# VectorE instead of GpSimd splits the queries and keys of batch 1 in layer 1 into bfloat16 parts

## The chip, the cores and the metric

The kernel runs on one NeuronCore of a Trainium2 chip. The metric is the device time of one execution in microseconds, a median over several runs. TensorE is called PE in the profile, VectorE DVE, ScalarE ACT, GpSimd POOL; SyncE (SP) issues nearly all DMAs. PEld is PE's weight load. Each engine works through its own instruction list in order, and they meet at semaphores.

## The reference

Two layers on x of shape (4, 512, 256) in float32: batch, tokens, channels. Each layer is x = layernorm(x + attention(x)), then x = layernorm(x + ffn(x)).

Layer 0 has attention with 16 query and 4 key heads, RMS norm and rotary embedding, and a mixture of 8 experts (one per token) beside a shared expert. Layer 1 has causal attention with 16 heads of 16 channels and a dense MLP whose weights are 4-bit integers with scales, plus low-rank terms. The part of the change is the start of layer 1's attention:

```
qkv = x @ W_qkv.T + b_qkv
q, k, v = split(qkv, 3)              # to 16 heads of 16 channels
scores = einsum('bnqd,bnkd->bnqk', q, k) * 16 ** -0.5
scores = where(causal, -inf, scores)
attn = softmax(scores)
out = einsum('bnqk,bnkd->bnqd', attn, v)
```

## The kernel before

**Splitting into bfloat16 parts.** The scores are wanted to nearly float32 precision but computed with bfloat16 matmuls. A float32 tile is taken apart into three bfloat16 parts: part 0 is the value rounded to bfloat16, the remainder is the value less part 0, part 1 is the remainder rounded, part 2 is the remainder less part 1. The parts of Q and K are written to DRAM and read back stacked, six rows per channel (96 rows for 16 channels), so that one bfloat16 matmul of 96 rows holds the products of the parts that matter.

**Units of work.** The order of all work is written out by hand as one string of step names. Every engine goes through that same string and does its own share of each step. In layer 1, for batch b:

- `cX`: PE turns the rows of x, ACT copies them.
- `cQ0` to `cQ3`: PE makes a 128 x 512 tile (`products`, L676); even ones are Q, odd ones K; two halves of the heads. ACT evicts it twice (L1108), with the bias: once as float32 to `qf`, once as bfloat16 to part 0 of `cparts`. ACT's step waits until split i-2 is done, and from i = 2 on for the DMAs that wrote the parts of the same buffer to DRAM before.
- `cK0` to `cK3`: the split of tile i: subtract, copy, subtract. For batches 0, 2 and 3 it is on DVE (L1469 to L1471), for batch 1 on POOL (L1609 to L1613). SP then writes the parts to DRAM in three DMAs (L643) and after every second split reads the stacks back (L628); the second half of batch 1's stacks is read only in `cM0`.
- `max` (written `m`): PE makes one bank of scores of the row maxima's pass, with the causal mask added by a second matmul (L904, L906); DVE reduces it to the row maxima (L1496). A batch has 44 such steps, over 512 or 384 columns.
- `cm`: DVE copies the finished maxima into two bfloat16 parts (L1503, L1504). `cM`: PE turns them, ACT copies them (L1124), SP writes them by two DMAs as two more rows of the Q stacks (L650), so that the second pass subtracts the maximum within the matmul.
- `cattS`, `cattP`: the 16 attention steps of a batch: scores (L928), exponential on ACT (L1118), the triangle cleared on POOL (L1622), the product with the values (L941).
- `Wul`, `Wdl`: low-rank products added to the dequantised MLP weights; ACT evicts, POOL adds (L1598).

**Order around the change.** The maxima of batch 0 have nothing of layer 1's attention to hide behind and run in the open, with Q and K of batch 1 among them (`+` marks batch 1, `m` without sign batch 0):

```
cX m m m m +cQ0 +cK0 m m m m m m +cQ1 +cK1 m m m m m m +cQ2 +cK2
m m m m m m m +cQ3 +cK3 m m m Wdl0 m m m m Wdl1 m m m Wdl2 m (11 times)
cm0 +cV0 Wd3 >cL0 >cL1 cM0 Wdl3 +cV1 >cE0     then the attention steps of batch 0
```

Maxima of batch 0 take turns over four PSUM banks (`WIDE`), since the score banks are still free; all other steps of this kind share three (`UNITS`). PE waits before a maximum until DVE has reduced the one that had the bank (`take`). Maxima of batches 1 to 3 lie between attention steps of the batch before.

The semaphore `cparts_ready` counts finished splits of either engine. On POOL the three instructions of a split wait for each other by `pool_parts`; on DVE `link` does that.

Of the kernel before, what the change touches and what calls it, by code (L numbers as in the profile page):

```python
# [25 lines left out]
ALU = mybir.AluOpType  # L26
# [124 lines left out]
def post_ln_layers(nc, ins, out):  # L151
# [4 lines left out]
    with ExitStack() as ctx:  # L156
# [5 lines left out]
        def place(shape, dt=F32):  # L162

            n = int(np.prod(shape)) * (2 if dt == BF16 else 4)
            n = (n + 31) // 32 * 8
            at = top[0]
            top[0] += n
            assert top[0] <= words, (top[0] * 4, words * 4)
            ap = arena[:, at:at + n]
            if dt != F32:  # L170
                ap = ap.bitcast(dt)
            ap = ap[:, 0:int(np.prod(shape))]
            if len(shape) > 1:
                names = "abcd"[:len(shape)]
                ap = ap.rearrange(f"p ({' '.join(names)}) -> p {' '.join(names)}",
                                  **{x: s for x, s in zip(names[1:], shape[1:])})
            return ap
# [156 lines left out]
        cresid = place([S])  # L334
# [4 lines left out]
        cparts = place([2, 3, S], BF16)  # L339
        qf = [place([S])]  # L340
# [19 lines left out]
        def sem(name):  # L360
            return ctx.enter_context(nc.semaphore(name))
# [60 lines left out]
        cparts_ready = sem("cparts_ready")  # L422
# [2 lines left out]
        cs_stack = [[sem(f"cstacks_loaded{h}{i}") for i in range(2)] for h in range(HG)]  # L425
        m_parts = sem("max_parts_ready")
        s_m = sem("max_rows_loaded")
        pool_parts = sem("pool_parts_chain")
        kones = sem("k_ones_ready")
        x3_ready = sem("x3_ready")  # L430
        y_ready = sem("y_ready")
# [8 lines left out]
        def yrow_of(b):  # L440

            return c_a_t.rearrange("p c (h n) -> p (c h) n", n=C) if b == 1 else yrow
# [37 lines left out]
        def consumed(eng, step):  # L480

            if step[:2] == OPENING:
                eng.wait_ge(max_free[step[2] % WIDE], step[2] // WIDE + 1)
                return
            u = unit_no[step]
            eng.wait_ge(unit_free[u % UNITS], u // UNITS + 1)
# [648 lines left out]
        def _(v):  # L1135
# [98 lines left out]
            for step in a_steps:  # L1234
                n, b, i = step
# [199 lines left out]
            for step in c_steps:  # L1435
                n, b, i = step
# [21 lines left out]
                elif n == "cE":  # L1458
                    tiles = x_sb[:, NT * b:NT * b + NT, :]
                    normalise(tiles, tiles, 0, NT, x2_ready, 2 * b + 2)  # L1460
                elif n == "cK" and b != 1:

                    s = i % 2
                    consumed(v, ("cQ", b, i))
# [71 lines left out]
        @block.gpsimd  # L1536
        def _(pool):

            pool.wait_ge(score_ready, 1)
            pool.wait_ge(s_xs, 16 * (B - 1))  # L1540
            nc.gpsimd.tensor_tensor(xs, x_sb[:, NT * (B - 1):NT * B, :], score.unsqueeze(2).to_broadcast([P, NT, C]),  # L1541
                                    ALU.mult).then_inc(xs_ready, 1)
            consumed(pool, ("ID", 0, 0))
            pool.wait_ge(s_xs, 16 * B)
            for j in range(MT):
                if j == 2:
                    consumed(pool, ("D", B - 2, 0))
                    consumed(pool, ("D", B - 2, 1))
                    nc.gpsimd.memset(low_rank, 0.0).then_inc(zeroed, 1)
                if j >= 2:  # L1550
                    pool.wait_ge(xgt_ps, j - 1)
                nc.gpsimd.indirect_dma_start(out=xg[:, j % 2, :], out_offset=None, in_=xs_dram,
                                             in_offset=bass.IndirectOffsetOnAxis(ap=ids[:, j:j + 1], axis=0))\
                  .then_inc(xg_in[j % 2], 16)

            pool.wait_ge(s_nat, 16 * 10)
            nc.gpsimd.tensor_scalar(n_up, n_up.bitcast(I32), 7.5, None, ALU.subtract).then_inc(poolc, 1)
            pool.wait_ge(poolc, 1)
            up4 = n_up.rearrange("p r (k j) -> p (r k) j", j=BLOCK)
            nc.gpsimd.tensor_tensor(up4, up4, n_ups.rearrange("p r k -> p (r k)").unsqueeze(2)  # L1560
                                    .to_broadcast([P, NK * C // BLOCK, BLOCK]), ALU.mult).then_inc(deq, 1)
            pool.wait_ge(deq, 1)
            nc.gpsimd.tensor_scalar(n_dn, n_dn.bitcast(I32), 7.5, None, ALU.subtract).then_inc(poolc, 1)
            pool.wait_ge(poolc, 2)
            dn4 = n_dn.rearrange("p r (k j) -> p (r k) j", j=BLOCK)
            nc.gpsimd.tensor_tensor(dn4, dn4, n_dns.rearrange("p r k -> p (r k)").unsqueeze(2)
                                    .to_broadcast([P, 2 * HID // BLOCK, BLOCK]), ALU.mult).then_inc(deq, 1)
            pool.wait_ge(deq, 2)

            pool.wait_ge(y_st[0], 16 * (MT // 2 + 1))  # L1570
            pool.wait_ge(y_st[1], 16 * (MT // 2))
            pool.wait_ge(y_full, MT)

            def gather(b):
                for t in range(NT):
                    nc.gpsimd.indirect_dma_start(out=yrow_of(b)[:, t, :], out_offset=None, in_=yg_dram,
                                                 in_offset=bass.IndirectOffsetOnAxis(ap=slot_i[:, NT * b + t:NT * b + t + 1],
                                                                                     axis=0)).then_inc(gathered[b % 2], 16)

            gather(0)  # L1580
            gather(1)
            for step in c_steps:
                n, b, i = step
                if n == "cL" and i == 1 and b == 1:

                    pool.wait_ge(x2_ready, 2)
                    gather(2)
                if n == "cP" and i == 1 and b == 0:

                    pool.wait_ge(x2_ready, 2 * B - 2)  # L1590
                    gather(B - 1)
                if n in ("Wul", "Wdl"):
                    k = low_steps.index(step)
                    consumed(pool, (n[:2], 0, i))
                    consumed(pool, step)
                    dst = (w_up[:, i // 2, 512 * (i % 2):512 * (i % 2 + 1)] if n == "Wul" else
                           w_dn[:, 2 * i:2 * i + 2, :].rearrange("p r n -> p (r n)"))
                    nc.gpsimd.tensor_tensor(dst, low_sum[k % 2], dst, ALU.add).then_inc(low_added, 1)  # L1598
                if n == "Wdl" and i < 2:
                    consumed(pool, ("cX", 0, i))  # L1600
                    pool.wait_ge(s_bias, 48)
                    rows = x_sb[:, 2 * i:2 * i + 2, :]
                    nc.gpsimd.tensor_tensor(rows, rows, bo_b.unsqueeze(1).to_broadcast([P, 2, C]), ALU.add).then_inc(o_bias, 1)
                if n == "cK" and b == 1:

                    t = i % 2
                    consumed(pool, ("cQ", b, i))
                    pool.wait_ge(cparts_ready, 4 * b + i)
                    nc.gpsimd.tensor_tensor(cresid, qf[t], cparts[:, t, 0, :], ALU.subtract).then_inc(pool_parts, 1)  # L1609
                    pool.wait_ge(pool_parts, 2 * i + 1)  # L1610
                    nc.gpsimd.tensor_copy(cparts[:, t, 1, :], cresid).then_inc(pool_parts, 1)
                    pool.wait_ge(pool_parts, 2 * i + 2)
                    nc.gpsimd.tensor_tensor(cparts[:, t, 2, :], cresid, cparts[:, t, 1, :], ALU.subtract)\  # L1613
                      .then_inc(cparts_ready, 1)
                elif n == "cattS":

                    k = head0 * B + headc * b + i
                    kt = i % NT
                    pool.wait_ge(exp_done[0], k + 1)
                    pool.wait_ge(exp_done[1], k + 1)  # L1620
                    diag = cprobs[:, i % 2, :, P * kt:P * (kt + 1)]
                    nc.gpsimd.affine_select(out=diag, in_=diag, compare_op=ALU.is_ge, fill=0.0, base=0,  # L1622
                                            pattern=[[0, 4], [1, P]], channel_multiplier=-1).then_inc(masked, 1)
# [35 lines left out]
def build(nc, arrays):  # L1659
    args = {n: nc.dram_tensor(f"in_{n}", a.shape, mybir.dt.from_np(a.dtype), kind="ExternalInput").ap()  # L1660
            for n, a in arrays.items()}
    out = nc.dram_tensor("out_0", (B, S, C), F32, kind="ExternalOutput").ap()
    post_ln_layers(nc, args, out)
# [24 lines left out]
```

## Time and profile before

| | us |
|---|---|
| median of 3 runs | 808.87 (807.51 to 809.41) |
| profiled execution | 804.52 |
| its span | 802.8 |
| PE busy | 755.4 (94%) |
| DVE busy | 446.9 (56%) |
| ACT busy | 398.7 (50%) |
| POOL busy | 126.8 (16%) |

The span is the time from the first to the last instruction of the profiled execution. Busy times overlap between engines. Times in rows are microseconds from the start of the span.

### The profile page before, as it was taken

What the parts mean: (1) busy time and instruction counts of PE and PEld (TensorE: products, weight loads), DVE (VectorE), ACT (ScalarE), POOL (GpSimd) and SP (SyncE); (2) the same over time, 40 slices, a digit from 0 to 9 for tenths busy, and PEclk for the clock granted to TensorE, in tenths of its full rate; (3) what the DMA queues carried; (4) which work ended last, traced back from release to release, by engine and by line L of the source; (5) the groups of instructions that cost most, each with busy time, mean ns of one, the idle gap of its engine ahead of it and who ended that gap; (6) DMA issues with size and microseconds to landing.
All of it is one profiled execution on the core that took longest, in us unless ns stands there. A gap on an engine that the chain in (4) does not pass through costs nothing. (4 is left out here: it accounts for less than half of the span.)

```text
span 802.8 us, 12486 instructions
## 1 busy us (share of the span) xinstructions
PE 755.4 (94%) x4393; PEld 446.3 (56%) x4394; DVE 446.9 (56%) x1194; ACT 398.7 (50%) x593; POOL 126.8 (16%) x135
## 2 busy tenths in 40 slices
PE   8899999999999999999999897989989998999996
PEld 4323434444434589999977554435445644653685
DVE  4663744565354722222228798939685667563464
ACT  3499775786595154454525325465333453146230
POOL 0000000000000131111563372223101110022100
PEclk9999999999999999999999999989999999999999
DMA  7668116105106262111123882005600280000000
GB/s 230 182 204 280 43 35 191 51 27 155 42 27 218 72 183 76 46 52 46 39 70 109 242 260 81 2 2 153 189 1 3 79 234 6 26 1 27 0 27 27
DMA packets 53822, 75.03 MB, mean 93 GB/s; under 512 B 7926, under 2 KB 45082, under 8 KB 53386
## 3 DMA queue, kind: packets, MB, share of 16 engines
q1 hardware_dynamic: 51900, 69.26, 28.0%
q0 software_dynamic: 1872, 5.11, 2.4%
q8 instruction: 30, 0.49, 0.3%
q14 instruction: 20, 0.16, 0.1%
HBM read 46.57 MB, written 27.66 MB: 92 GB/s over the span
## 5 line engine op out<-in xcount | busy, mean ns | idle before, releaser
L676 PE MATMUL ps<-arena 128*128 128x256 f32 (+3 forms) x1084 | 315.8, 439 | 5.6 <-DVE arena L1217 1.4
L676 PEld LDWEIGHTS ps<-arena 128*128 128x128 f32 x1084 | 196.1, 190 | 87.9 <-issue 55.4
L1003 ACT ACTIVATE arena<-ps 128x1024 f32<-128x1024 f32 x128 | 124.1, 1029 | 25.6 <-PE ps L744 25.3
L1118 ACT ACTIVATE arena<-ps 128x1024 f32<-128x1024 f32 (+3 forms) x128 | 82.9, 702 | 99.0 <-PE ps L928 98.8
L1496 DVE TENSOR_REDUCE arena<-ps 128x1 f32<-128x384 f32 (+3 forms) x176 | 100.5, 634 | 26.0 <-PE ps L906 25.3
L806 PE MATMUL ps<-arena 128*128 128x128 f32 x736 | 89.4, 275 | 0.6 <-DVE arena L1228 0.6
L806 PEld LDWEIGHTS ps<-arena 128*128 128x128 f32 x736 | 87.4, 192 | 2.4 <-issue 1.3
L1622 POOL TENSOR_SCALAR_AFFINE_SELECT arena<-arena 128x512 f32<-128x512 f32 x64 | 42.5, 664 | 218.4 <-ACT arena L1118 218.4
L904 PE MATMUL ps<-arena 96*128 96x128 bf16 (+3 forms) x256 | 62.3, 306 | 12.0 <-DVE arena L1496 7.3
L744 PE MATMUL ps<-arena 96*128 96x512 bf16 x256 | 69.7, 382 | 4.2 <-ACT arena L1003 2.7
L758 PE MATMUL ps<-arena 128*32 128x512 f32 x512 | 68.8, 604 | 0.3 <-ACT arena L1010 0.3
L744 PEld LDWEIGHTS ps<-arena 96*128 96x128 bf16 x256 | 17.8, 97 | 77.5 <-ACT arena L1003 40.7
L928 PE MATMUL ps<-arena 98*128 98x512 bf16 (+3 forms) x256 | 47.8, 307 | 4.9 <-ACT arena L1118 2.7
L941 PE MATMUL ps<-arena 128*32 128x128 f32 (+3 forms) x512 | 49.0, 454 | 2.8 <-POOL arena L1622 1.8
L906 PE MATMUL ps<-arena 128*128 128x128 bf16 x256 | 49.5, 223 | 0.0
L904 PEld LDWEIGHTS ps<-arena 96*128 96x128 bf16 x256 | 25.3, 99 | 39.0 <-DVE arena L1496 19.6
L928 PEld LDWEIGHTS ps<-arena 98*128 98x128 bf16 x256 | 18.2, 98 | 47.6 <-issue 31.4
L1541 POOL TENSOR_TENSOR arena<-arena 128x1024 f32<-128x1024 f32 x1 | 1.9, 1895 | 265.7 <-DVE arena L1326 265.7
L815 PE MATMUL ps<-arena 128*128 x184 | 43.4, 379 | 0.0
L1031 ACT ACTIVATE arena<-ps 128x512 f32<-128x512 f32 x23 | 13.7, 597 | 55.8 <-PE ps L806 55.8
L668 PE MATMUL ps<-arena 128*128 128x128 f32 (+3 forms) x237 | 33.9, 280 | 7.7 <-DVE arena L1270 3.2
L668 PEld LDWEIGHTS ps<-arena 128*128 128x128 f32 (+3 forms) x237 | 28.1, 141 | 20.5 <-issue 8.6
(160 smaller groups left out, 755.3 us busy)
## 6 DMA issues: line engine op xcount, KB each, us to landing
arena<-stacks_dram SPq DMA_DIRECT2D x32, 384.0 KB, 6.3
arena<-in_gate_up_proj SPq DMA_DIRECT2D x8, 1024.0 KB, 9.3
stacks_dram<-arena SPq DMA_DIRECT2D x16, 384.0 KB, 3.7
arena<-in_down_proj SPq DMA_DIRECT2D x8, 512.0 KB, 9.0
stacks_dram<-arena SPq DMA_DIRECT2D x16, 256.0 KB, 4.0
q_stacks_dram<-arena SPq DMA_DIRECT2D x8, 384.0 KB, 3.3
arena<-q_stacks_dram SPq DMA_DIRECT2D x8, 384.0 KB, 4.8
arena<-q_stacks_dram SPq DMA_DIRECT2D x4, 768.0 KB, 5.8
```

Source lines behind the costliest of these rows:

```text
L668: last = nc.tensor.transpose(dst[0:rows, col:col + n], src, idn)
L676: last = nc.tensor.matmul(dst[0:rows, lo:hi], a, w, start=(n == 0), stop=(n == len(pairs) - 1))
L744: last = nc.tensor.matmul(ps[:, g, :], k_stack[0:STACK, b % 2, hg, cols(kt)], q_stack[0:STACK, b % 2, 4 * hg + g, :], start=True, stop=True)
L758: last = nc.tensor.matmul(ps[32 * g:32 * g + 32, 4, :], v_aug[:, kt, hg, :], (probs0, probs1)[i % 2][:, g, :], start=(kt == 0), stop=(kt = ...
L806: last = nc.tensor.matmul(ps[:, 2 * half + up, cols(f)], of_expert[:, up, c, cols(f)], xg_t[:, half, c, :], start=(c == 0), stop=(c == 1))
L904: nc.tensor.matmul(dst[:, w * g:w * (g + 1)], cq_stack[0:STACK, b % 2, h0 + g, cols(qt)], ck_stack[0:STACK, b % 2, h0 + g, 0:w], start=Tru ...
L906: last = nc.tensor.matmul(dst[:, w * g + P * qt:w * (g + 1)], identb, negmask, start=False, stop=True, skip_group_check=True)
L928: last = nc.tensor.matmul(ps[:, g, P * kt:S], ck_stack[0:STACK + 2, b % 2, h, cols(kt)], cq_stack[0:STACK + 2, b % 2, h, P * kt:S], start= ...
L941: last = nc.tensor.matmul(ps[32 * g:32 * g + 32, 4, P * kt:S], cv_aug[:, b % 2, kt, 4 * hg + g, :], cprobs[:, i % 2, g, P * kt:S], start=( ...
L1003: nc.scalar.activation(probs[:, 2 * p:2 * p + 2, :], ps[:, 2 * p:2 * p + 2, :], ACT.Exp)\
L1118: nc.scalar.activation(cprobs[:, i % 2, 2 * p:2 * p + 2, P * kt:S], ps[:, 2 * p:2 * p + 2, P * kt:S], ACT.Exp).then_inc(exp_done[p], 1)
L1496: nc.vector.tensor_reduce(mneg[:, qt, h0:h0 + nh], filled(v, step)[:, 0:nh * w].rearrange("p (h n) -> p h n", n=w), AX.X, ALU.max, negate= ...
```

## The change

For batch 1 the split moves from POOL's list to DVE's. DVE's branch for `cK` no longer leaves out batch 1, POOL's branch and its semaphore go. The string of steps, the buffers and the DMAs stay.

```diff
-        pool_parts = sem("pool_parts_chain")
...
-                elif n == "cK" and b != 1:
+                elif n == "cK":

                     s = i % 2
                     consumed(v, ("cQ", b, i))
...
-                if n == "cK" and b == 1:
-
-                    t = i % 2
-                    consumed(pool, ("cQ", b, i))
-                    pool.wait_ge(cparts_ready, 4 * b + i)
-                    nc.gpsimd.tensor_tensor(cresid, qf[t], cparts[:, t, 0, :], ALU.subtract).then_inc(pool_parts, 1)
-                    pool.wait_ge(pool_parts, 2 * i + 1)
-                    nc.gpsimd.tensor_copy(cparts[:, t, 1, :], cresid).then_inc(pool_parts, 1)
-                    pool.wait_ge(pool_parts, 2 * i + 2)
-                    nc.gpsimd.tensor_tensor(cparts[:, t, 2, :], cresid, cparts[:, t, 1, :], ALU.subtract)\
-                      .then_inc(cparts_ready, 1)
-                elif n == "cattS":
+                if n == "cattS":
```

## Rows read from the trace of the kernel before

**Rows 1.** The page, part 1: busy time, share of the span and instructions

```profile
PE 755.4 (94%) x4393; PEld 446.3 (56%) x4394; DVE 446.9 (56%) x1194; ACT 398.7 (50%) x593; POOL 126.8 (16%) x135
```

**Rows 2.** Busy time by stretches, chosen around idle PE and lower clock

```profile
core 0: us, PE busy (x) PEld busy (x) DVE busy (x) ACT busy (x) POOL busy (x), PEclk, DMA share, GB/s
...
450.50:452.38 1.88, 0.01 (x1) 0.01 (x1) 1.82 (x2) 1.10 (x3) 1.67 (x2) 1.00 1.01 326
452.90:456.20 3.30, 3.30 (x21) 2.53 (x19) 2.14 (x4) 0.60 (x1) 0.00 (x0) 0.50 0.79 276
456.30:482.00 25.70, 24.88 (x150) 14.28 (x148) 22.70 (x42) 6.85 (x11) 17.81 (x17) 1.00 0.81 246
...
528.87:530.64 1.77, 0.00 (x1) 0.01 (x1) 0.00 (x0) 0.00 (x0) 0.30 (x1) 1.00 0.07 19
531.40:538.20 6.80, 6.71 (x33) 2.83 (x32) 2.46 (x4) 4.70 (x6) 1.27 (x2) 0.50 0.00 0
538.20:802.80 264.60, 244.02 (x1407) 143.90 (x1405) 163.49 (x456) 98.70 (x160) 34.80 (x50) 1.00 0.19 59
```

**Rows 3.** Timeline of DVE: start, us, what, idle before and its end

```profile
454.06 2.35 DVE L1496 TENSOR_REDUCE arena<-ps 128x4 f32<-128x512 f32 x4 [1.74 <-PE ps L906]
458.05 3.28 DVE L1496 TENSOR_REDUCE arena<-ps 128x1 f32<-128x384 f32 x6 [1.63 <-PE ps L906]
461.66 3.41 DVE L1496 TENSOR_REDUCE arena<-ps 128x1 f32<-128x512 f32 x6 [0.33 <-PE ps L906]
465.43 4.01 DVE L1496 TENSOR_REDUCE arena<-ps 128x1 f32<-128x384 f32 x7 [0.36 <-PE ps L906]
469.97 11.69 DVE L1496 TENSOR_REDUCE arena<-ps 128x2 f32<-128x512 f32 x21 [0.53 <-PE ps L906]
481.79 0.20 DVE L1503 CAST arena<-arena 128x64 bf16<-128x64 f32 x1
```

**Rows 4.** Timelines of ACT, SP's queue and PE behind the maxima

```profile
482.74 0.59 ACT L1124 ACTIVATE arena<-ps 32x512 bf16<-32x512 bf16 x1
...
483.35 1.24 SPq L650 DMA_DIRECT2D arena<-arena  x2
...
486.19 1.04 PE L928 MATMUL ps<-arena 98*128 98x512 bf16 x4 [0.30 <-DMA arena<-arena]
```

**Rows 5.** Timeline of POOL: the first split of batch 1, its ends

```profile
459.17 1.16 POOL L1609 TENSOR_TENSOR arena<-arena 128x512 f32<-128x512 f32 x1 [7.00 <-ACT arena L1108]
...
461.08 1.16 POOL L1613 TENSOR_TENSOR arena<-arena 128x512 bf16<-128x512 f32 x1
```

**Rows 6.** Timeline of DVE: the last split of batch 0 and what follows

```profile
442.24 0.68 DVE L1469 TENSOR_TENSOR arena<-arena 128x512 f32<-128x512 f32 x1
442.96 0.43 DVE L1470 CAST arena<-arena 128x512 bf16<-128x512 f32 x1
443.42 0.69 DVE L1471 TENSOR_TENSOR arena<-arena 128x512 bf16<-128x512 f32 x1
444.03 0.75 DVE L1480 TENSOR_TENSOR arena<-ps,arena 128x256 f32<-128x256 f32 x2
```

**Rows 7.** Timelines of PE and ACT around Q and K of batch 1

```profile
458.51 0.22 PE L906 MATMUL ps<-arena 128*128 128x128 bf16 x1
...
459.12 0.39 PE L904 MATMUL ps<-arena 96*128 96x512 bf16 x1
...
459.41 1.93 PE L676 MATMUL ps<-arena 128*128 128x512 f32 x4
461.18 0.38 PE L904 MATMUL ps<-arena 96*128 96x512 bf16 x1
...
457.82 1.27 ACT L1108 ACTIVATE arena<-ps,arena 128x512 f32<-128x512 f32 x2 [4.12 <-PE ps L676]
461.38 1.26 ACT L1108 ACTIVATE arena<-ps,arena 128x512 f32<-128x512 f32 x2 [2.29 <-PE ps L676]
467.69 1.27 ACT L1108 ACTIVATE arena<-ps,arena 128x512 f32<-128x512 f32 x2 [5.04 <-DMA stacks_dram<-arena]
```

**Rows 8.** Timeline of PE, a maximum of batch 2 behind a wait

```profile
596.51 0.39 PE L904 MATMUL ps<-arena 96*128 96x512 bf16 x1 [1.55 <-DVE arena L1496]
```

## The prediction

> **What bounds the kernel now.** I read the page first, then busy time by stretches, then the timelines of single engines over the opening of layer 1. TensorE (PE) is busy 94% of the span, VectorE (DVE) 56%, GpSimd (POOL) 16% [rows 1]. From such averages the move looks like one from an idle engine to a half idle one. The chain that ended last is no help, since it is followed back only to 718.89 us; the change sits near 460 us. So the stretch has to be read itself. Between 456.30 and 482.00 DVE is busy 22.70 of 25.70 us and POOL 17.81 [rows 2], whose columns are the stretch, its length, the busy us of PE, PEld, DVE, ACT and POOL with their counts, the granted clock, the DMA share and GB/s. PE's 24.88 there is the modelled end of short matmuls, not full work.
>
> The timeline of DVE shows what the 22.70 are: the 44 maxima of batch 0, in runs of 4, 6, 6, 7 and 21, with DVE idle only 1.63, 0.33, 0.36 and 0.53 us ahead of the last four runs. Each of these four pauses is PE making Q0, K0, Q1 or K1 of batch 1 (the steps cQ0 to cQ3) between the maxima, and DVE then waits for the first maximum behind it. The last 21 run without a pause to 469.97 + 11.69 = 481.66, and the copy of the row maxima follows at 481.79 [rows 3]. What hangs from it is a plain chain: ScalarE's (ACT) copy of the turned maxima at 482.74, their two DMAs at 483.35, and the first score matmul of batch 0 at 486.19, which had waited for that DMA [rows 4]. Every later step of PE is ordered behind it. DVE too goes on in one list: after the copy of the maxima come the values and the layer norm, then the maxima of batch 1. So whatever delays the 44th maximum delays both engines by as much, and PE is busy 244.02 of the 264.60 us behind 538.20 [rows 2], with nothing that arrives from outside on a date of its own.
>
> **What the change does, part by part.**
> Removed: 12 instructions on POOL, three per split; the first split runs there from 459.17 to 461.08 + 1.16 = 462.24, 3.07 us [rows 5]. Four make 12.3 us, all off the path: POOL's next customer is the low rank sum of the weights, needed only in the MLP after the first attention. Worth nothing.
>
> Added: the same 12 on DVE. Batch 0's splits are there already: 0.68, 0.43 and 0.69 us, and from the start of the first to the start of the next step 444.03 - 442.24 = 1.79 [rows 6]. Four are 7.16 us, in an engine with no room for them.
>
> Moved: the waits. Split i stands in DVE's list behind the maxima that stand ahead of it and must wait until ACT has written both copies of its Q or K. Queued behind the waiting split are the next maxima; behind these PE, since the maxima of batch 0 have four PSUM banks. Worked through:
> - The fourth maximum ends at 454.06 + 2.35 = 456.41. ACT's pair for the first Q ends at 457.82 + 1.27 = 459.09 [rows 3, 7]. The split starts about 459.13, idle 2.72; the next maxima start at 460.92 instead of 458.05.
> - Six maxima take 3.28 and end at 464.20. PE has filled four banks by 458.5 and gets the fifth and sixth only as DVE frees them, about 0.5 us apart (3.28/6), so at 461.9; its last maximum takes 0.29 (459.12 to 459.41), so the next K's matmuls start at 462.2, not at 459.41. From that start to ACT's is 461.38 - 459.41 = 1.97, ACT takes 1.26 [rows 3, 7]: done at 465.5. The second split is at 465.52, idle 1.32; maxima 11 to 16 run from 467.31 to 470.72.
> - The same with the two wide maxima ahead (0.6 each, 2.35/4): Q at 468.8, ACT done 472.0, split 472.08 (idle 1.36), seven maxima 473.87 to 477.88 (4.01).
> - Q of the fourth, behind three freed banks, at 475.85; ACT done 479.1, split 479.13 (idle 1.25), 21 maxima 480.92 to 492.61.
> That is 492.61 - 481.66 = 10.95 later: 7.16 for the splits and 6.65 - 2.86 = 3.79 of more idling, since ACT's pass now stands in DVE's way where POOL used to wait for it.
>
> One cover disappears too, at no price. ACT's third pair waited for the DRAM write of the first parts until 467.69 [rows 7]; now the matmuls for it end near 470.6 and the parts are ready 1.2 us sooner, so that wait goes, but it is not what DVE waited for before. SP's queue gets the parts at about 461.0, 467.4, 474.0 and 481.0. The second half of batch 1's stacks is loaded after the maxima's DMA in both kernels, and is first used 22 maxima into the attention.
>
> **The clock.** PE now stands idle between the eighth and ninth maximum from 458.5 to about 461.5, and again about 2.5 to 2.8 us in each of the next two rounds (from 465.4 to 467.9, from 471.6 to 474.4). In the trace idle gaps of 1.88 and 1.77 us, at 450.50 and 528.87, each were followed by a stretch at a granted clock of 0.50, 1.2 GHz (452.90 to 456.20, and 531.40 to 538.20) [rows 2]; a gap of 1.55 us at 595 was not [rows 8]. Where the clock is at its lower level while one of the last three Q or K is made, its matmuls take 1.77 us more (461.18 - 459.41 [rows 7], once again), and that comes straight out of the idle time of DVE. None is +0, all three +5.3; I take half, 2.7, as the gaps are longer than both that cost the clock but may fall so that the rise comes back in time. The sum is 10.95 + 2.7 = 13.6 us.
> The Trainium skill, "TensorE: Matmul & The Clock Gate", section "A second HAM failure mode: psum-queue depth-cycling", describes such a kernel: PE idles for a moment between groups as it goes through its PSUM banks, and its clock swings between the levels. By that rule the change costs 10.95 and something on top; without it 10.95. The trace agrees as far as its two gaps go.
>
> **Rivals.**
> 1. Only DVE's own time counts: the extra idling is covered because PE runs ahead further than I think. +7.16, 816.0 us. For it: PE did run ahead in the old order, with pauses of only 0.33 to 0.53. Against it: four banks are four banks.
> 2. The clock stays low through the whole stage: maxima that keep PE busy at 1.2 GHz too. 10.95 + 5.3 and one to four more for the maxima, about +19, 828 us. For it: four gaps in a row. Against it: PE, busy 3.30 of 3.30 us from 452.90 at the lower level, was at the higher again behind 456.30 [rows 2].
> 3. Faster: the chain Q, split, write to DRAM, next Q sets the end, not the maxima. Its place is ACT's third pair, idle 5.04 us until the write of POOL's first parts had landed [rows 7]. DVE's split takes 1.8 against 3.07 us; the most that can be had is that wait, -5.0, 803.8 us. It decides from the point at which DVE idles longer per round than a split lasts, 1.79; before the change it idles 0.33 to 0.53 in three of four [rows 3], so it is unlikely.
> The Trainium skill, "GPSIMD Engine Reference", section "4.1 Engine selection", gives elementwise work to VectorE, as GpSimd is about half as fast with two inputs. By that rule alone this change would be the third rival; the trace has the ratio (1.16 against 0.69) and also the full DVE.
> 4. Nothing: the delay is made up behind 486 by slack that I don't see; 808.9.
>
> **How the numbers follow.** The profiled execution took 804.52 us with a span of 802.8; with the sum it would take 818.1. The median of the runs is 808.87, 4.35 above it; I add the same difference: 822.5. Chances: forecast 0.80 (its own range 818 to 826.5), rival 1 0.07, rival 2 0.07, rival 3 0.03, rival 4 0.03. The range 816 to 827 takes in rival 1 and most of the clock's doubt. Of a change under 0.2% this kernel's times can't tell anything: faster 0.03, same 0.03, slower 0.94.
>
> **What would show it.** In the profile after: 16 splits of DVE, none of POOL, the four new ones at 1.8 us each; ahead of each DVE idles for ACT, 2.7 us and then 1.2 to 1.4 (more where the clock is down); the copy of the maxima at 492 to 497 instead of 481.79; the first score matmul 4.4 us behind that as before; from there on everything later by the same amount, within 2 us. PE idle gaps of 2.5 to 3 us near 459, 466 and 472, with one to three stretches at 0.50 that weren't there. Wrong would be: a copy of the maxima before 490 (rival 1), the shift shrinking behind it (rival 4), or DVE idling long ahead of maxima rather than of splits.

## The result and the profile after

| | before | after |
|---|---|---|
| median of 3 runs, us | 808.87 | 823.70 (821.22 to 826.17) |
| profiled execution, us | 804.52 | 821.22 |
| its span, us | 802.8 | 819.5 |
| mean granted clock | 0.990 | 0.980 |

The medians differ by 14.8 us (1.83%), where 13.6 had been forecast, and the time lies in the range. The ratio computed from the single runs, after to before, is 1.0213, 95% interval 1.0184 to 1.0242, a little more than the quotient of the medians; with three runs each the two measures need not agree. The same kernel run six times below comes out at 1.0180.

The timeline of DVE over the same stage (start, us, what, idle before and what ended it) answers to [rows 3, 6]. Line numbers are one lower, since a line has gone.

```profile
449.13 4.20 DVE L1182 TENSOR_SCALAR arena<-arena 128x256 f32<-128x256 f32 x4
454.66 2.35 DVE L1495 TENSOR_REDUCE arena<-ps 128x4 f32<-128x512 f32 x4 [1.32 <-PE ps L905]
458.53 0.69 DVE L1468 TENSOR_TENSOR arena<-arena 128x512 f32<-128x512 f32 x1 [1.52 <-ACT arena L1107]
459.25 0.43 DVE L1469 CAST arena<-arena 128x512 bf16<-128x512 f32 x1
459.72 0.69 DVE L1470 TENSOR_TENSOR arena<-arena 128x512 bf16<-128x512 f32 x1
460.33 3.27 DVE L1495 TENSOR_REDUCE arena<-ps 128x1 f32<-128x384 f32 x6
466.22 0.69 DVE L1468 TENSOR_TENSOR arena<-arena 128x512 f32<-128x512 f32 x1 [2.62 <-ACT arena L1107]
...
468.01 3.40 DVE L1495 TENSOR_REDUCE arena<-ps 128x1 f32<-128x512 f32 x6
474.37 0.69 DVE L1468 TENSOR_TENSOR arena<-arena 128x512 f32<-128x512 f32 x1 [2.95 <-ACT arena L1107]
...
476.17 4.00 DVE L1495 TENSOR_REDUCE arena<-ps 128x1 f32<-128x384 f32 x7
483.79 0.69 DVE L1468 TENSOR_TENSOR arena<-arena 128x512 f32<-128x512 f32 x1 [3.62 <-ACT arena L1107]
...
485.59 11.57 DVE L1495 TENSOR_REDUCE arena<-ps 128x2 f32<-128x512 f32 x21
497.29 0.19 DVE L1502 CAST arena<-arena 128x64 bf16<-128x64 f32 x1
```

The reader is to see two things. Each split fills DVE for 1.80 us (458.53 to 460.33), and ahead of each DVE now waits for ScalarE: 1.52, 2.62, 2.95 and 3.62 us. The copy of the maxima comes at 497.29, not at 481.79 [rows 3]. Between executions everything up to this point shifts by a microsecond or so, so I measure the stage from the last layer norm instruction ahead of it: 448.13 in the kernel before (a row of four of 4.19 us there), 449.13 here. From there to the copy of the maxima it was 33.66 us and is 48.16: **the stage is 14.50 us longer**. It adds up: 7.16 for the splits; pauses of 10.71 instead of 2.85, 7.86 more; less 0.40, as the first four maxima end that much sooner in this execution, and 0.12, as the last 21 run in 11.57 instead of 11.69.

Busy time by stretches (stretch, length, PE, PEld, DVE, ACT, POOL with counts, granted clock, DMA share, GB/s) answers to [rows 2]:

```profile
462.30:465.50 3.20, 3.20 (x9) 1.19 (x8) 1.29 (x3) 0.58 (x1) 0.00 (x0) 0.50 1.03 288
465.70:468.90 3.20, 1.16 (x15) 0.85 (x13) 2.62 (x5) 0.48 (x1) 0.00 (x0) 1.00 0.20 70
469.10:472.40 3.30, 3.09 (x6) 1.36 (x6) 2.31 (x5) 0.00 (x0) 0.00 (x0) 0.50 0.71 236
472.50:475.80 3.30, 1.53 (x10) 0.61 (x8) 1.36 (x3) 1.26 (x2) 0.00 (x0) 1.00 0.36 106
475.90:482.60 6.70, 5.83 (x19) 2.72 (x20) 4.27 (x8) 0.11 (x1) 0.00 (x0) 0.50 1.00 283
...
510.10:513.30 3.20, 3.20 (x19) 1.02 (x18) 1.60 (x4) 0.47 (x2) 0.00 (x0) 0.50 0.00 0
```

Three stretches at 0.50 (1.2 GHz) lie between 462 and 483, where the kernel before had none from 456.30 to 482. The timeline of PE shows what stands ahead of them: the fifth maximum after each Q or K waits for DVE to free its bank.

```profile
460.94 0.39 PE L903 MATMUL ps<-arena 96*128 96x512 bf16 x1 [2.79 <-DVE arena L1495]
468.75 0.34 PE L903 MATMUL ps<-arena 96*128 96x384 bf16 x1 [2.04 <-DVE arena L1495]
...
476.77 0.61 PE L903 MATMUL ps<-arena 96*128 96x512 bf16 x1 [2.74 <-DVE arena L1495]
```

And what comes of them is that the matmuls of the next K or Q take 1.7 to 1.9 times as long (1.93 us as shown in [rows 7]):

```profile
461.68 3.20 PE L675 MATMUL ps<-arena 128*128 128x512 f32 x4
...
469.75 3.28 PE L675 MATMUL ps<-arena 128*128 128x512 f32 x4
...
478.73 3.72 PE L675 MATMUL ps<-arena 128*128 128x512 f32 x4
```

Behind the stage nothing takes the loss back. The first score matmul is 4.40 us behind the copy of the maxima in both kernels (501.69 here; [rows 3, 4] before). From the copy to the end it is 322.2 us here and 321.0 before; in the 1.2 us more lies one more stretch at 0.50, at 510.10. With 1.0 us ahead of the stage and 14.5 in it these are the 16.7 us between the two spans.

### The profile page after: what moved, and what is told of

Read it like the earlier page. It is cut to its first block and busy times, and to the rows that moved or that the text cites. A ratio compares the mean times of both kernels' runs of the same rounds, so it can differ in the third digit from the quotient of the medians.

```text
span 819.5 us, 12486 instructions
## 1 busy us (share of the span) xinstructions
PE 762.8 (93%) x4393; PEld 447.9 (55%) x4394; DVE 452.9 (55%) x1206; ACT 398.5 (49%) x593; POOL 115.1 (14%) x123
## 5 line engine op out<-in xcount | busy, mean ns | idle before, releaser
L675 PE MATMUL ps<-arena 128*128 128x256 f32 (+3 forms) x1084 | 319.7, 443 | 5.6 <-DVE arena L1216 1.4
L903 PE MATMUL ps<-arena 96*128 96x128 bf16 (+3 forms) x256 | 63.8, 311 | 21.1 <-DVE arena L1495 16.7
L1107 ACT ACTIVATE arena<-ps,arena 128x512 f32<-128x512 f32 (+1 forms) x32 | 20.2, 683 | 40.0 <-PE ps L675 39.1
```

The source lines that it names most:

```text
L675: last = nc.tensor.matmul(dst[0:rows, lo:hi], a, w, start=(n == 0), stop=(n == len(pairs) - 1))
L903: nc.tensor.matmul(dst[:, w * g:w * (g + 1)], cq_stack[0:STACK, b % 2, h0 + g, cols(qt)], ck_stack[0:STACK, b % 2, h0 + g, 0:w], start=Tru ...
```

## The experiments

Each ratio is to runs of the kernel before on the same chip (medians 806.13 and 806.24 us there). The column "over before" is the difference of the medians; the ratio is computed from the single runs, and where the two part, as in "waits only" (0.61% is 4.9 us) and "first two splits" (1.00% is 8.1 us), the text gives both. Most intervals are 4 to 5 us wide, so differences of 3 us between two rows rest on the profiles more than on the medians. The rows "again", "splits late", "waits only" and "5 matmuls" were measured on one chip, the other four on another. "Stage" is the time from the last layer norm instruction to the copy of the maxima in the profiled execution, less the 33.66 us of the kernel before.

| kernel | over before, us | ratio, 95% interval | stage, us | its waits for ScalarE ahead of the four splits |
|---|---|---|---|---|
| changed kernel, again | 14.6 | 1.0180 (1.0151 to 1.0208) | 14.0 | 1.52, 2.76, 2.81, 1.49 |
| splits late | 10.2 | 1.0125 (1.0091 to 1.0160) | 8.3 | none |
| waits only | 5.7 | 1.0061 (1.0038 to 1.0085) | 6.1 | 3.19, 1.36, 1.79, 3.15 |
| PE filled, 5 matmuls | 15.1 | 1.0177 (1.0146 to 1.0209) | 14.7 | 3.20, 2.06, 2.27, 1.93 |
| PE filled, 2 matmuls | 11.6 | 1.0143 (1.0117 to 1.0169) | 11.2 | 1.52, 1.35, 1.43, 1.49 |
| first two splits on DVE | 9.2 | 1.0100 (1.0067 to 1.0133) | 9.5 | 3.19, 3.44 |
| splits late, last one sooner | 7.3 | 1.0089 (1.0056 to 1.0122) | 6.3 | none |
| before, Q and K later | 0.9 | 1.0007 (0.9987 to 1.0028) | -0.4 | (on POOL) |

**The changed kernel again.** No edit.

> The changed kernel once more, beside the other three on one chip. Theory: the loss has three terms, DVE's own time (7.2 us), DVE's extra waiting for ScalarE at the splits at full clock (3.8 us), and the clock stretches at 0.50 in which the last three of Q and K are made (4 to 5 us); so 14 to 16 us over the kernel before, with low stretches near 462, 469 and 476 again, at times that may differ by run, and single runs that differ by 2 us or more. Rival: the clock stretches were an accident of one execution; then this comes out at about 11 us over.

14.6 us over, in the middle of what was expected. Its stretches at 0.50 began at 461.0, 467.9 and 484.9: twice in the same places; the third came after the last K, and the wait ahead of the last split was then 1.49 us, not 3.62. So the low clock is no accident of one execution, but which K or Q it hits changes from one profiled execution to the other. Single runs went from 819.36 to 822.96.

**The splits late.** DVE still does all four, but comes to each only when ScalarE is long done.

```diff
-m m m m m m +cQ1 +cK1 m m m m m m +cQ2 +cK2 m m m m m m m +cQ3 +cK3 m m m Wdl0 m m m m Wdl1
+m m m m m m +cK0 +cQ1 m m m m m m +cK1 +cQ2 m m m m m m m +cK2 +cQ3 m m m Wdl0 m m m +cK3 m Wdl1
```
(Excerpts of the string, with its lines joined. `+cK0` goes from its old place too.)

> Only the place of the splits on DVE differs from the changed kernel: each stands behind the six or seven maxima that follow its Q or K, just ahead of the next one, so ScalarE has long delivered when DVE comes to it. Theory: the waiting and with it PE's long idle gaps go; DVE's time of 7.2 us stays, and the pauses of 0.33 to 0.53 us that DVE had before are taken up by it: 6 to 7 us over the kernel before, 8 to 9 under the changed one, no low stretch between 456 and 480. Rival (it is the load on DVE and the clock, wherever the splits stand): 11 us or more over the kernel before.

The waits for ScalarE went, but the cost was above the 6 to 7 us expected and below the 11 or more of the rival: 8.3 us in the stage, 10.2 in the median. Missed too was "no low stretch": one ran from 470.6 to 474.1, and the matmuls of the last K took 3.25 us in it. Here that cost DVE almost nothing: its pause there was 0.35 us. So in this stage the low clock costs by way of DVE's wait for ScalarE, and where that wait isn't in DVE's way it costs little. The profile shows where part of the rest is (timeline of DVE, then of POOL):

```profile
477.27 0.98 DVE L1468 TENSOR_TENSOR arena<-arena 128x512 f32<-128x512 f32 x1
478.29 1.37 DVE L1469 CAST arena<-arena 128x512 bf16<-128x512 f32 x1
479.69 1.63 DVE L1470 TENSOR_TENSOR arena<-arena 128x512 bf16<-128x512 f32 x1
```

```profile
477.66 1.71 POOL L1602 TENSOR_TENSOR arena<-arena 128x512 f32<-128x512 f32 x1
479.34 1.44 POOL L1597 TENSOR_TENSOR arena<-arena 128x512 f32<-128x512 f32 x1
480.74 1.71 POOL L1602 TENSOR_TENSOR arena<-arena 128x512 f32<-128x512 f32 x1
```

The last split lay beside POOL's additions and took 3.98 us instead of 1.80. A low stretch from 484.3 on hit the value products behind the maxima as well: DVE waited 1.26 us for PE there, which the stage doesn't count.

**The last split sooner.** The same kernel, with `+cK3` behind the first maximum after `+cQ3`, ahead of POOL's additions. The diff is against the kernel with the splits late.

```diff
-+cK2 +cQ3 m m m Wdl0 m m m +cK3 m Wdl1
++cK2 +cQ3 m +cK3 m m Wdl0 m m m m Wdl1
```

> As the kernel with the splits on DVE placed late, but the last of them stands behind the first maximum after the last K, before POOL begins with the low rank sums. In that kernel the last split lasted 0.98, 1.37 and 1.63 us beside POOL's additions, against 0.68, 0.43 and 0.69 alone. Theory: all four splits at 1.8 us, the 44th maximum 6 to 7 us later than in the kernel before instead of 8.3, and 1.5 to 2.5 us less than that kernel. Rival (the longer instructions were no matter of POOL): the last split is as long as it was.

```profile
474.92 0.69 DVE L1468 TENSOR_TENSOR arena<-arena 128x512 f32<-128x512 f32 x1
475.65 0.43 DVE L1469 CAST arena<-arena 128x512 bf16<-128x512 f32 x1
476.11 0.69 DVE L1470 TENSOR_TENSOR arena<-arena 128x512 bf16<-128x512 f32 x1
476.72 10.98 DVE L1495 TENSOR_REDUCE arena<-ps 128x2 f32<-128x512 f32 x20
```

The split is back to 1.80 us and the stage at 6.3, as expected; in the median 2.9 us less than its sister (10.2 less 7.3), against 1.5 to 2.5 expected, with intervals that overlap; the profiles show 2.0 us, the split itself 2.2. This is the price of the splits' own time without waiting for ScalarE: 7.3 us in the median, against 7.16 for four splits.

**The waits only.** POOL does the splits; DVE waits where the changed kernel splits, and does nothing.

```diff
+                elif n == "cK":
+                    consumed(v, ("cQ", b, i))
```

> The kernel before, POOL does the splits, but DVE waits at the places where the changed kernel splits until ScalarE has delivered that Q or K, and then does nothing. Theory: the waiting by itself costs 3 to 5 us (DVE idle 2.7 us and then 1.2 to 1.4 each, against 1.63, 0.33, 0.36, 0.53), with PE gaps of about 1 us and no new low stretch. Rival (waiting was only a consequence of the low clock): within 1 us of the kernel before.

5.7 us by the medians and 4.9 by the ratio, at or just above the upper end of the expected 3 to 5 and far from the rival. The profiled execution, the slowest of the nine (815.83 us), shows what can make it more: a low stretch came after all, at 471.7, and the wait for the last K was 3.15 us. Ahead of it PE had been idle for only 1.30 us and then 0.24, ahead of the fifth and the seventh maximum of that round. So a wait alone costs, and the low clock is reached with shorter idle gaps than I thought. The first wait of 3.19 us has a low stretch of its own, from 454.65 to 458.06. At full clock the price should be about 2.9 us, an estimate from the four waits of 5.8 us in the kernel with two idle matmuls below, less the 2.85 of before.

**PE filled.** Idle matmuls (of `ones` into PSUM bank 4, which nothing reads) ahead of the maxima that wait for a bank; five in the first kernel, two in the second, where `range(5)` is `range(2)`.

```diff
+                    if b == 0 and i in (8, 14, 20):
+                        for _ in range(5):
+                            nc.tensor.matmul(ps[:, 4, :], ones, ones.unsqueeze(1).to_broadcast([P, NT, P]), start=True, stop=True)
                     dst = take(pe, step)
```

> The changed kernel with five idle float32 matmuls of 512 columns (0.43 us each, 2.1 us in all) on PE into a free PSUM bank ahead of maxima 9, 15 and 21 of batch 0, where PE stood idle 2.0 to 2.8 us. Nothing that counts waits for them. Theory: the low stretches near 462, 469 and 476 go, DVE's waits at the splits fall to 1.2 to 1.4 us, and the time to about 11 us over the kernel before, 4 to 5 under the changed one. Rival 1 (all of the extra waiting came of the clock): 7 to 8 us over the kernel before. Rival 2 (the clock is not on the path): no faster than the changed kernel.

This was sized wrongly: each float32 matmul of 512 columns is two records of 0.45 us, so five lasted 4.51 us. Between 458.1 and 546.8 there was no low stretch, but the fill itself now held up the next maxima and Q: DVE waited 0.40, 0.42 and 0.32 us within the maxima and 2 us at the splits. It was no faster than the changed kernel, which is what rival 2 says, but the fill's own cost is in that time, so it decides neither rival. Hence the second one:

> As the kernel with five idle matmuls, but with two (0.9 us each, 1.8 us in all, as that run showed them: ten records in 4.51 us): short enough to end before DVE frees the bank that PE waits for (gaps of 2.0 to 2.8 us). Theory: no low stretch or at most one between 456 and 484, DVE idle 1.2 to 1.4 us ahead of each of the last three splits at full clock, the 44th maximum 11 to 12 us later than in the kernel before (measured from the last layer norm instruction ahead of them), and 3 to 4 us less than the changed kernel in the median. Rival (the clock is not on the path of this stage): the 44th maximum as late as in the changed kernel, 14 us.

```profile
458.29 0.69 DVE L1471 TENSOR_TENSOR arena<-arena 128x512 f32<-128x512 f32 x1 [1.52 <-ACT arena L1110]
...
464.71 0.69 DVE L1471 TENSOR_TENSOR arena<-arena 128x512 f32<-128x512 f32 x1 [1.35 <-ACT arena L1110]
...
471.35 0.69 DVE L1471 TENSOR_TENSOR arena<-arena 128x512 f32<-128x512 f32 x1 [1.43 <-ACT arena L1110]
...
478.64 0.69 DVE L1471 TENSOR_TENSOR arena<-arena 128x512 f32<-128x512 f32 x1 [1.49 <-ACT arena L1110]
```

```profile
456.30:482.30 26.00, 20.75 (x101) 9.83 (x100) 19.93 (x37) 5.66 (x9) 2.34 (x2) 1.00 0.77 224
482.50:485.70 3.20, 3.20 (x11) 2.04 (x10) 2.15 (x5) 0.60 (x1) 0.57 (x2) 0.50 0.42 142
```

The granted clock was 1.00 over the whole stretch of the four splits, all Q and K at 1.93 us, the waits what they are at full clock, and the median 3.0 us below the changed kernel run again (11.6 against 14.6 over the kernel before). The intervals of the two just overlap and the chips differ, so the medians alone leave this open; the profiles agree with it, with waits of 5.79 us in sum against 8.58 and a stage of 11.2 against 14.0. More work on PE made the stage shorter. Rival 1 of the kernel with five (all of the extra waiting came of the clock) is out as well: at full clock the waits are still 2.94 us more than the pauses before. One low stretch, at 482.50, came behind the last split and cost two pauses of 1.05 and 0.41 us in the last maxima.

**Half of the change.** DVE splits the first Q and K, POOL the second pair.

```diff
-                elif n == "cK" and b != 1:
+                elif n == "cK" and (b != 1 or i < 2):
...
-                if n == "cK" and b == 1:
+                if n == "cK" and b == 1 and i >= 2:
...
```
(Not shown: POOL's two waits on `pool_parts` become `2 * i - 3` and `2 * i - 2`, as its first split is now the third.)

> Half of the change: DVE splits the first two of batch 1 (Q and K of the first half of the heads), POOL the last two. Theory: each split costs its 1.8 us, about 1.2 us of waiting, and what the clock adds: 44th maximum 6 to 7 us later, median 6 to 8 us over the kernel before. Rival (the loss comes once, from a delay of the first Q that runs through): 10 us or more over, or under 4.

9.2 us by the medians and 8.1 by the ratio, at or above the upper end of 6 to 8, and more than half of 14.6; the stage, at 9.5, was above the 6 to 7 expected. The profiled execution is the slowest of the six: the clock was at 0.50 from 453.8 to 457.2 and again from 460.6 for 6.8 us, the waits ahead of the two splits were 3.19 and 3.44 us, and DVE then stood 2.05 us more for PE ahead of the next maxima. The six runs lie between 810.52 and 818.70 us. The fastest has the highest mean clock (0.988) and the slowest the lowest (0.979), though in between 814.54 and 818.10 both go with 0.983. So the price per split is not a constant; that it hangs on where the low stretches fall is likely, but only one of the six has a profile. The rival of a single early delay is not excluded by this run alone (its interval goes from 5.4 to 10.7 us), but by the waits of all four splits in the changed kernel.

**The kernel before with Q and K four maxima later.**

```diff
-+cX0 +cX1 m m m m +cQ0 +cK0 m m m m m m +cQ1 +cK1 m m m m m m +cQ2 +cK2 m m m m m m m +cQ3 +cK3 m m m Wdl0
++cX0 +cX1 m m m m m m m m +cQ0 +cK0 m m m m m m +cQ1 +cK1 m m m m m m +cQ2 +cK2 m m m m m m +cQ3 +cK3 Wdl0
```
(Excerpts of the string, with its lines joined.)

> The kernel before, POOL does the splits, with Q and K of batch 1 four maxima later in the list: the first of them behind maximum 8 instead of 4, when PE has run ahead of DVE and DVE has maxima to go on with. Theory: DVE's pause of 1.63 us ahead of the fifth maximum goes, all else stays: 1 to 1.5 us faster than the kernel before, which is hardly to be told from none. Rival (POOL's splits end 5 us later and delay the stacks of batch 1 or the low rank sums): slower by 1 us or more.

No difference that can be measured (1.0007, 0.9987 to 1.0028). The pause didn't go, it moved: DVE was idle 1.15, 0.21, 0.47 and 1.09 us, 2.92 in all against 2.85. And what the stage gained, 0.4 us, was lost at once, by what the rival feared in part: POOL's additions come later, and the last of them lay beside the copy of the maxima, which took 1.13 us instead of 0.20 (timeline of DVE, then of POOL).

```profile
482.16 1.13 DVE L1503 CAST arena<-arena 128x64 bf16<-128x64 f32 x1
```

```profile
481.98 1.25 POOL L1598 TENSOR_TENSOR arena<-arena 128x512 f32<-128x512 f32 x1
```

No version beat the kernel before.

## Why the prediction was right, point by point

- **The stage is bounded by DVE, and the loss goes through to the end.** Right. Stage +14.5, rest +1.2 with one more low stretch; score matmul at the forecast 4.4 us behind the copy of the maxima, which came at 497.29, just past the forecast 492 to 497; 1.0 us of that was there ahead of the stage. Rival 4 is out: from the copy to the end nothing is made up.
- **Splits, 7.16 us.** Right: four of 1.80 in the profile, and 7.3 us in the median of the kernel in which they are nearly the only cost.
- **Waiting for ScalarE, 3.79 us at full clock.** Right in kind, 0.85 too high. In the kernel with two idle matmuls the waits are 1.52, 1.35, 1.43 and 1.49, in sum 5.79, which is 2.94 more than the pauses before. I had 1.32, 1.36 and 1.25 for the last three, and 2.72 for the first, because the low stretch at 452.90 delayed the first Q in the execution that I read; where no low stretch came there it is 1.52 (the changed kernel twice, and with two idle matmuls). With the clock low from 453.8 or 454.7 on it is 3.19 or 3.20, in three kernels. Rival 1 (only DVE's own time) is out by this and by the waits-only kernel.
- **The clock, 2.7 us, taken as half of 5.3.** The mechanism was right, the term mis-sized: all three hits came, and the waits of 10.71 less the 5.79 at full clock are 4.92 us in the profiled execution, near the 5.3 that the prediction gave for three hits and then halved. The gaps of PE ahead of them were 2.79, 2.04 and 2.74 us, the middle one shorter than the 2.5 to 2.8 that I had worked out. In the medians it is 3.0 us (14.6 less 11.6 over the kernel before), where the profile of the kernel run again has two hits rather than three. The too high waiting and the too low clock term cancelled in part. That in the profiled executions the low stretches among the splits go when PE's gaps are filled, and the long waits with them, is shown; that some other effect of the fill gave a part of the 3 us isn't excluded by a run of its own, but the difference of the two stages (2.8 us) is all in DVE's pauses. Rival 2 (low through the whole stage) did not happen: between the hits the clock was at 1.00. The Trainium skill ("TensorE: Matmul & The Clock Gate", "A second HAM failure mode: psum-queue depth-cycling") describes a PE that idles briefly between groups of matmuls as it goes through its PSUM banks, with a clock that swings between its levels. The trace after agrees: pauses of 2.79, 2.04 and 2.74 us ahead of maxima that wait for a bank, each with a stretch at 0.50 behind it and 1.00 between them.
- **Rival 3, the chain over DRAM.** Out. ScalarE's third pair no longer waited for a DMA (its wait at 473.07 was for PE), and nothing got faster for it.
- **POOL's time is worth nothing.** Right: with POOL's busy time down from 126.8 to 115.1 us nothing came back.
- **The total.** Partly luck. The profiled execution was forecast at 818.1 and took 821.22, 3.1 us more, as the clock term was too small. To come from it to the median I added 4.35 us, the difference in the kernel before; in the kernel after it was 2.48. The two misses cancelled in part, and so 822.5 met 823.70 better than its terms deserve.

## What to carry to other kernels

Moving work from a slow idle engine to a fast one pays only if the fast one is idle in that very stage; the share over the span says nothing about it. An instruction that moves takes its waits along: placed straight behind its producer in a full engine's list it waited about 1.4 us at full clock ahead of 1.8 us of work, and up to 3.6 us where the clock was low; placed one round later it waited not at all. And if other engines wait in turn, count what their idle gaps do to PE's clock.

## What was not expected of the hardware

- DVE's elementwise instructions on two SBUF operands grew from 0.68 and 0.69 us to 0.98 and 1.63, and the cast between them from 0.43 to 1.37, beside POOL's additions, which themselves grew from 1.26 to 1.71; moved out of POOL's way they were back at 0.69, 0.43 and 0.69. The Trainium skill ("SBUF — State Buffer", "Who interferes with whom") describes a port pair that the two engines share and that one of them locks for a whole instruction; these rows agree with that. The three instructions of DVE end 0.55, 0.29 and 0.54 us behind the end of the POOL instruction ahead of them (477.70, 479.37 and 480.78), each a little less than its time alone: they look like turns taken, not like two engines that slow each other evenly. The copy of 1.13 us in the last kernel ended 0.06 us behind POOL's addition. The maxima, which DVE reads from PSUM, ran beside the same additions without change (11.57 us for 21).
- The length of a single gap doesn't tell whether the clock falls. In the changed kernel gaps of 2.79, 2.04 and 2.74 us were each followed by a stretch at 0.50; in the same kernel run again the one of 2.74 us was not, and one of 1.82 us was; in the waits-only kernel 1.30 us, with 0.24 behind it, was enough, where 1.55 us was not in [rows 8]. In the changed kernel the gap of 1.20 us ahead of 508.70 was followed by the low stretch at 510.10, and the same gap ahead of 493.21 in the kernel before by none.
- Even the kernel before varies from 803.98 to 809.88 us over 14 runs on one chip. A difference of 1 us, as was looked for with the last kernel, can't be read from a single pair.
